# Two graph layers on one core: score chunks moved behind aggregations, masks behind residuals, and a new preparation of the first graph

## The chip, the core and the metric

The kernel runs on one core of a Trainium2 chip. Its engines work side by side and wait for one another by semaphores: TensorE (PE in the profile, its weight loads PEld), VectorE (DVE), ScalarE (ACT), GpSimd (POOL) and SyncE (SP), which issues most of the DMAs. The metric is the time of one execution on the device in microseconds.

## What is computed

Sixteen graphs of 1024 nodes with 256 features go through two layers. The reference, cut to what matters (the adjacency here holds 0 and 1 alone, so that layer 0 uses only `a0`):

```python
# layer 0
e0 = leaky(einsum('bid,bjd->bij', h * a0[:, 0], h))        # leaky: x if x >= 0 else 0.2 x
alpha = sigmoid(where(adj == 1, e0, -max_float))
x = layernorm(h + einsum('bij,bjd->bid', alpha, h) + bias)
# layer 1
Hh = einsum('bni,io->bno', x, W)
logits = (Hh @ a_src)[:, :, None] + (Hh @ a_dst)[:, None, :]
e = where(adj != 0, exp(-leaky(logits)), 0)
x = layernorm(x + elu(einsum('bnm,bmo->bno', e, Hh) / sum(e)))
```

## The kernel before

**Tiles.** A graph's 1024 nodes are 8 tiles t of 128. A product in float32 is made of three products of rounded parts (`split_products`: high x high, low x high, high x low). ScalarE makes the high parts by a rounding copy, GpSimd or VectorE the low parts by a subtraction: `high_x`/`low_x` of x, `high_xT`/`low_xT` of the turned x (its copy scaled by a0 is gT), `high0`/`low0` and `high1`/`low1` of the coefficients of the layers, `keep_H`/`low_H` of the projection.

**Layer 0.** Scores are symmetric, so only the blocks on and above the diagonal are made, in 12 chunks of up to 512 columns (`CHUNKS`): chunks 0 to 2 are rows 7, 6, 5; 3 and 4 row 0; 5 and 6 row 1; 7 and 8 row 2; 9 and 10 row 3; 11 row 4. TensorE makes a chunk in one of two banks (`scores_chunk`), ScalarE writes 0.2 times it (`scale_scores`), VectorE takes the maximum with the bank (`leaky_scores`), ScalarE a tanh over the row (`tanh_row`). The blocks below the diagonal are transposed on TensorE (`mirror`). VectorE forms the coefficients of block t by two kinds of products with the transposed codes: `mask0_below` from the mirrored bank, and `mask0_rest` from `score`. Then high and low part, and `aggregate0`, 24 products of TensorE per tile. The result goes through `residual0`, `stats0`, `moments0` (VectorE), `power0` (GpSimd: variance to 1/sigma) and `norm0` (VectorE), which leaves x1.

**Layer 1.** x1 is turned (`transpose_x1`, `keep_x1T`) and projected (`project`, with two more columns of `W_ext` that hold W a_src and W a_dst). `mask1_tiles` makes the coefficients of several tiles, `aggregate1` sums them, `row_inverse`, `elu_parts` (ScalarE: exponential, then relu), `residual1`, `stats1`, `moments1`, `power1` (GpSimd), `norm1` (ScalarE) and a DMA finish a tile.

**Order.** No scheduler is at work: each engine's instructions stand in the order in which its function `graph(b, prev, nxt)` writes them. Graph 0 and the last one stand by themselves, graphs 1 to 14 run in a loop. Layer 1 of a graph is laced with layer 0's scores of the next, and at the end of graph b ("the border") the masks, high and low parts 0 to 3 of graph b+1 are made between the residuals 4 to 7 of graph b. All semaphores count up; a wait names the count that it needs. Before the first graph there is a preparation: constants, weights, x, the scores of graph 0 and its first four blocks.

The part of the first preparation that makes the two columns of `W_ext` was done on VectorE (`extend_weights`): a product with a row of `a` spread over the partitions (`a_bc`) and a sum, for two columns and two halves.

## Time and profile before

| | us |
|---|---|
| median of 3 runs | 1290.91 |
| lowest, highest | 1290.22, 1291.21 |
| profiled execution, its time | 1292.38 |
| profiled execution, span of its instructions | 1290.6 |
| granted clock of TensorE, mean | 0.992 |

| engine | busy us | share of the span |
|---|---|---|
| PE | 1212.5 | 94% |
| PEld | 1135.5 | 88% |
| POOL | 1045.2 | 81% |
| DVE | 997.1 | 77% |
| ACT | 988.9 | 77% |

The profiled execution's own time is 1.5 us above the median. A row of the timeline gives start, duration, engine, line of the kernel, operation, what it writes and reads with shapes, the number of merged instructions, and in brackets the idle time before it with what ended it. A line is that of a helper, so the tile names tell what it works on: line 1253 is the first of the three products of a step, for scores and aggregations alike.

### The profile page before, as it was taken

How to read it: one execution, taken by the hardware profiler on the slowest of the kernel's cores; microseconds unless marked ns; L12 is line 12 of the kernel's file. 1: busy time of each engine (PE TensorE's matmuls, PEld its weight loads, DVE VectorE, ACT ScalarE, POOL GpSimd, SP SyncE). 2: the span in 40 equal slices, each digit the busy share in tenths (PEclk: the TensorE clock that was granted, in tenths of full speed). 3: DMA queues.
4: the chain of work that ended last, by engine and by line, in shares of the span. 5: the costliest groups of instructions: out<-in, count | busy, mean ns of one | idle time of the engine just before them, and what ended most of it. 6: DMA issues, size and time to landing. Idle time of an engine off the chain costs nothing.

```text
span 1290.6 us, 29789 instructions
## 1 busy us (share of the span) xinstructions
PE 1212.5 (94%) x8898; PEld 1135.5 (88%) x8898; DVE 997.1 (77%) x2499; ACT 988.9 (77%) x2290; POOL 1045.2 (81%) x1052
## 2 busy tenths in 40 slices
PE   5899999999999999999999999999999999999985
PEld 4789899898998989899898988989898898988875
DVE  4678778787877878778787877878778787878855
ACT  4677878778787887878788787887878788787763
POOL 2779797887988889797887988889797887978864
PEclk9999999999999999999999999999999999999988
DMA  9467390854828366381854828366381854818301
GB/s 192 90 118 137 58 178 27 154 106 86 166 40 150 78 131 129 57 164 39 154 106 78 174 37 148 83 129 126 62 162 42 154 106 70 182 34 147 56 9 36
DMA packets 223634, 135.31 MB, mean 105 GB/s; under 512 B 141168, under 2 KB 207088, under 8 KB 223600
## 3 DMA queue, kind: packets, MB, share of 16 engines
q1 hardware_dynamic: 188528, 84.57, 28.0%
q0 software_dynamic: 35072, 50.34, 26.0%
q8 instruction: 15, 0.25, 0.1%
q14 instruction: 19, 0.16, 0.0%
HBM read 101.32 MB, written 16.78 MB: 92 GB/s over the span
## 4 chain that ended last, share of the span: by engine, by line
DVE 34%; POOL 31%; issue 22%; PE 6%; ACT 4%; DVEq 1%; POOLq 1%; DMA 0%; ACTq 0%
POOL coef_lo L394 9%; POOL coef_lo L402 8%; DVE coef L1010 6%; DVE coef L940 5%; POOL rstd L434 3%; DVE stats L1052 3%; DVE reluP L1047 3%; DVE xt_bank L1044 3%; DVE stats L958 2%; DVE coef L931 2%; DVE resid L953 2%; DVE gT_lo L884 2%; POOL var_eps L431 2%; POOL coef_lo L408 2%; POOL h_lo L385 2%
## 5 line engine op out<-in xcount | busy, mean ns | idle before, releaser
L394 POOL TENSOR_TENSOR coef_lo<-coef,coef_hi 128x1024 fp32r<-128x1024 f32 x128 | 307.0, 2405 | 57.4 <-DVE x L970 32.1
L1253 PE MATMUL acc_bank<-h_hi,coef_hi 128*128 128x256 f32 x1024 | 302.5, 295 | 16.6 <-ACT reluP L702 13.9
L402 POOL TENSOR_TENSOR coef_lo<-coef,coef_hi 128x1024 fp32r<-128x1024 f32 (+1 forms) x128 | 294.5, 2308 | 11.5 <-ACT coef_hi L636 11.1
L1253 PE MATMUL acc_bank<-H_hi,coef_hi 128*128 128x258 f32 x1024 | 296.0, 289 | 7.4 <-ACT reluP L702 5.4
L1254 PE MATMUL acc_bank<-H_lo,coef_hi 128*128 128x258 f32 x1024 | 290.6, 284 | 0.0
L1255 PE MATMUL acc_bank<-H_hi,coef_lo 128*128 128x258 f32 x1024 | 290.2, 283 | 0.0
L1255 PE MATMUL acc_bank<-h_hi,coef_lo 128*128 128x256 f32 x1024 | 285.9, 279 | 0.0
L1254 PE MATMUL acc_bank<-h_lo,coef_hi 128*128 128x256 f32 x1024 | 285.8, 279 | 0.0
L1253 PEld LDWEIGHTS acc_bank<-h_hi,coef_hi 128*128 128x128 f32 x1024 | 193.7, 189 | 26.7 <-issue 22.4
L1010 DVE SCALAR_TENSOR_TENSOR coef<-tr_bank,E_col,codeT 128x256 f32<-128x256 f32 (+1 forms) x384 | 193.0, 565 | 24.2 <-POOL coef_lo L402 21.7
L1253 PEld LDWEIGHTS acc_bank<-H_hi,coef_hi 128*128 128x128 f32 x1024 | 194.3, 190 | 11.2 <-issue 8.3
L1254 PEld LDWEIGHTS acc_bank<-H_lo,coef_hi 128*128 128x128 f32 x1024 | 195.1, 191 | 0.6
L1255 PEld LDWEIGHTS acc_bank<-H_hi,coef_lo 128*128 128x128 f32 x1024 | 195.1, 191 | 0.0
L1254 PEld LDWEIGHTS acc_bank<-h_lo,coef_hi 128*128 128x128 f32 x1024 | 193.8, 189 | 1.5
L1255 PEld LDWEIGHTS acc_bank<-h_hi,coef_lo 128*128 128x128 f32 x1024 | 193.2, 189 | 0.0
L626 ACT ACTIVATE coef_hi<-coef 128x1024 fp32r<-128x1024 f32 x128 | 136.2, 1064 | 73.0 <-DVE coef L940 73.0
L588 ACT ACTIVATE score<-lg_bank 128x128 f32<-128x128 f32 (+2 forms) x192 | 94.7, 493 | 86.3 <-PE lg_bank L1255 82.6
L1253 PE MATMUL lg_bank<-hT_hi,gT_hi 128*128 128x384 f32 (+3 forms) x384 | 144.6, 377 | 7.5 <-DVE score L893 4.5
L940 DVE SCALAR_TENSOR_TENSOR coef<-score,codeT 128x512 f32<-128x512 f32 (+1 forms) x192 | 147.9, 797 | 2.0 <-POOL coef_lo L394 0.4
L616 ACT ACTIVATE watch_junk<-codeT,half_cols 128x1024 bf16<-128x1024 bf16 x128 | 147.9, 1155 | 0.6
L1358 PE MATMUL hh_bank<-W_ext,x1T 128*128 128x258 f32 x512 | 139.6, 395 | 7.6 <-ACT x1T L653 4.9
L893 DVE TENSOR_TENSOR score<-lg_bank,score 128x128 f32<-128x128 f32 (+2 forms) x192 | 103.5, 553 | 38.6 <-ACT score L588 38.6
(91 smaller groups left out, 2814.7 us busy)
## 6 DMA issues: line engine op xcount, KB each, us to landing
code_nat<-in_adj POOLq DMA_DIRECT2D x128, 256.0 KB, 4.8
x_raw<-in_x SPq DMA_DIRECT2D x16, 1024.0 KB, 6.5
xb<-bias_bc SPq DMA_DIRECT2D x16, 1024.0 KB, 8.7
xb<-in_x POOLq DMA_DIRECT2D x16, 1024.0 KB, 12.2
out<-x SPq DMA_DIRECT2D x128, 128.0 KB, 2.0
codeT<-code_nat SPq DMA_TRANSPOSE x128, 3.5
W_ext<-in_L_gnn_W SPq DMA_DIRECT2D x1, 256.0 KB, 3.9
x1T<-in_L_gnn_a SPq DMA_DIRECT2D x1, 256.0 KB, 5.1
```

What stands on the lines that cost most here:

```text
L394: nc.gpsimd.tensor_tensor(coef_lo[:, t % 4, :, :], blocks(coef[:, t % 4, :]), f32(coef_hi[:, t % 4, :, :]), ALU.subtract).then_inc(S.lo0, 1)
L402: nc.gpsimd.tensor_tensor(coef_lo[:, t % 4, j0:NT, :], blocks(coef[:, t % 4, j0 * P:N]), f32(coef_hi[:, t % 4, j0:NT, :]), ALU.subtract).t ...
L588: nc.scalar.activation(score_at(J, c0, c1), lg_bank[k % 2][:, 0:(c1 - c0) * P], ACT.Copy, scale=SLOPE).then_inc(F.scaled, 1)
L616: nc.scalar.activation(watch_junk[:, :], codeT[:, t, :], ACT.Square, bias=neg_half[:, :], accum_out=watch_sum[:, t:t + 1]).then_inc(F.code ...
L626: nc.scalar.activation(coef_hi[:, t % 4, :, :], blocks(coef[:, t % 4, :]), ACT.Copy).then_inc(S.hi0, 1)
L893: nc.vector.tensor_tensor(score_at(J, c0, c1), lg_bank[k % 2][:, 0:(c1 - c0) * P], score_at(J, c0, c1), ALU.max).then_inc(F.leaky, 1)
L940: ins = nc.vector.scalar_tensor_tensor(blocks(coef[:, t % 4, j0 * P:j1 * P]), score[:, 0:j1 - j0, at:at + P], 1.0, blocks(codeT[:, t, j0 * ...
L1010: ins = nc.vector.scalar_tensor_tensor(coef[:, at:at + count, J * P:(J + 1) * P], G, E_col[:, J:J + 1], codeT[:, t:t + count, J * P:(J + 1 ...
L1253: nc.tensor.matmul(dst, lhs_hi, rhs_hi, start=first, stop=False)
L1254: nc.tensor.matmul(dst, lhs_hi, rhs_lo, start=False, stop=False)
L1255: return nc.tensor.matmul(dst, lhs_lo, rhs_hi, start=False, stop=last)
L1358: ins = nc.tensor.matmul(hh_bank[:, 0:HC], x1T[:, t % 2, dt, :], W_ext[:, dt, :], start=dt == 0, stop=dt == KD - 1)
```

## The change

It has four parts.

1. **Score chunks.** In layer 1 of graph b, TensorE made chunk 8 behind aggregation 0, chunks 9 and 10 behind aggregation 1 and chunk 11 behind aggregation 2. Now chunks 9, 10 and 11 stand one each behind aggregations 1, 2 and 3. `scale_scores` and `leaky_scores` of them move along.
2. **Masks and high parts at the border.** Row inverse 7 stands behind moments 6, ahead of `mask0_rest` 2; residual 7 ahead of both mask products of block 3. On ScalarE, `high0` 2 and 3 stand behind the relu of tile 7. The high parts of x of the next graph move back by a few places.
3. **Masks 3 and 4 of layer 1's first group** stand behind `norm0` 7 and chunk 2's maximum.
4. **The preparation of the first graph.** x is loaded in three pieces, the last tiles first; the four turned pairs have four banks (`x_bank`) and are not held up by one another; scores start with the first pair. VectorE rounds two of the high parts of x. The columns `a_col` are loaded by ScalarE's queue. W is turned on TensorE and multiplied with both halves of `a` at once (`turn_weights`, `weights_by_a`). The bias is added by GpSimd (`add_bias_pair`) instead of by two DMAs. `mirror` 3 stands behind aggregation 0. The transposing DMAs of codes 4 to 7 stand behind the load of graph 1's x. Two semaphores are merged into others.

The diff, cut to its core (left out: the declarations, waits of the same meaning, `add_bias_pair` and its callers' waits as told above):

```diff
-                    sp.dma_start(a_col[:, k, :], ak.rearrange("(c p) o -> p (c o)", p=P)).then_inc(cols_loaded, 16)
+            for q in range(2):
+                tiles = slice(NT - 2 * q - 2, NT - 2 * q)
+                sp.dma_start(x_raw[:, tiles, :], x_v[0, :, tiles, :]).then_inc(x_part[q], 16)
...
             sp.wait_ge(weights_loaded, 16 * N_WEIGHT_DMAS)
-            sp.sem_inc(past, 1)
-            fill_bias()
+            sp.wait_ge(F.xT, 4)
             sp.wait_ge(F.h_lo, 4)
-            sp.wait_ge(F.xT, 4)
+            sp.wait_ge(F.xb_bias, 4)
             sp.sem_inc(past, 1)
             load_x(F, 1)
+            for t in range(4, NT):
+                turn_codes(0, t, True)
             with sp.Fori(0, LAST - 1) as b:
                 graph(b, True)
...
+            pool.wait_ge(weights_loaded, 16 * N_WEIGHT_DMAS)
+            pool.wait_ge(F.x_loaded, 16)
             for c in range(4):
-                low_x(F, 0, c)
...
-                if nxt:
-                    high_x(F, b + 1, 0)
                 keep_H(F, b, 6, prev, False)
                 keep_x1T(F, b, 7, prev)
-                if nxt:
-                    high_x(F, b + 1, 1)
+                high1_begin(b)
+                if nxt:
                     scale_scores(b + 1, 4)
                 keep_H(F, b, 7, prev, False)
                 ends_H(F, b)
                     scale_scores(b + 1, 6)
...
                         scale_scores(b + 1, 8)
-                        high_x(F, b + 1, 3)
+                        high_x(F, b + 1, 2)
                     if t >= 1:
                         elu_parts(F, b, t - 1)
                     if t == 1:
                         high1(F, b, 4)
                         if nxt:
-                            scale_row(b + 1, 3)
+                            high_x(F, b + 1, 3)
+                            scale_scores(b + 1, 9)
                         high1(F, b, 5)
+                    if nxt and t in (2, 3):
+                        scale_scores(b + 1, 8 + t)
                     if nxt and t == 2:
-                        scale_row(b + 1, 4)
                         tanh_row(b + 1, 0)
                     if t in (3, 4):
                         high1(F, b, t + 3)
-                    if t + 3 >= NT and nxt:
-                        high0(F, b + 1, t + 3 - NT, True)
+                    if nxt and t in (5, 6):
+                        high0(F, b + 1, t - 5, True)
+                    if nxt and t == NT:
+                        high0(F, b + 1, 2, True)
                     if nxt and 3 <= t:
                         tanh_row(b + 1, t - 2)
+                    if nxt and t == NT:
+                        high0(F, b + 1, 3, True)
                     if nxt and t == NT:
                         tanh_row(b + 1, NT - 1)
                     if t in (4, 6, 8):
                         norm1(F, b, t - 4)
                         norm1(F, b, t - 3)
...
             scale_scores(0, 3)
             scale_scores(0, 4)
-            high_x(F, 0, 1)
-            for J in range(4):
-                scale_scores(0, 5 + 2 * J)
-                if J >= 2:
-                    high0(F, 0, J - 2, False)
+            tanh_row(0, 0)
+            scale_scores(0, 5)
+            scale_scores(0, 6)
+            tanh_row(0, 1)
+            for J in range(2, 5):
+                scale_scores(0, 2 * J + 3)
+                high0(F, 0, J - 2, False)
+                if J < 4:
+                    scale_scores(0, 2 * J + 4)
                 tanh_row(0, J)
-                if J < 3:
-                    scale_scores(0, 6 + 2 * J)
-                if J < 2:
-                    high_x(F, 0, J + 2)
-            high0(F, 0, 2, False)
-            tanh_row(0, 4)
...
-                        ins.then_inc(setup_step, 1)
+            def high_x_first(q):
+                dve.wait_ge(x_part[q], 16)
+                tiles = x_pair(F, 0, q)
+                nc.vector.tensor_copy(h_hi[:, tiles, :], x_raw[:, tiles, :]).then_inc(F.h_hi, 1)
+            def keep_W_turned():
+                dve.wait_ge(setup_step, 6)
+                nc.vector.tensor_copy(W_turned, xt_bank[:, :].rearrange("p (c k) -> p c k", c=KD)).then_inc(setup_step, 1)
+            def extend_weights():
+                dve.wait_ge(setup_step, 8)
+                nc.vector.tensor_copy(W_ext[:, :, D:HC],
+                                      hh_bank[:, 0:2 * KD].rearrange("p (c k) -> p c k", c=KD)).then_inc(weights_ready, 1)
             def low_xT(S, b, c, general):
...
                         mask1_tiles(b, 0, 4, 0, 3)
                     if t == 8:
                         low_H(F, b, 5)
-                        mask1_tiles(b, 0, 4, 3, EDGE)
                         keep_watch(b, prev)
                         if prev:
                             keep_range(b - 1)
                     if nxt and 6 <= t:
                         leaky_scores(b + 1, t - 6)
+                mask1_tiles(b, 0, 4, 3, EDGE)
                 if nxt:
                     leaky_scores(b + 1, 3)
                 low_H(F, b, 6)
...
-                    if t >= 3:
+                    if 3 <= t < 7:
                         row_inverse(F, b, t, prev)
-                    if t >= 4 and nxt:
+                    if 4 <= t < 7 and nxt:
                         mask0_below(b + 1, t - 4, True)
+                    if 4 <= t < 6 and nxt:
                         mask0_rest(b + 1, t - 4)
                     residual1(F, b, t, prev)
                     stats1(F, b, t)
                     moments1(F, b, t)
+                    if t == 6:
+                        row_inverse(F, b, 7, prev)
+                        if nxt:
+                            mask0_rest(b + 1, 2)
+                    if t == 7 and nxt:
+                        mask0_below(b + 1, 3, True)
+                        mask0_rest(b + 1, 3)
                     if t < 2:
                         row_inverse(F, b, t + 1, prev)
                     if t == 0:
                         if nxt:
-                            leaky_row(b + 1, 3)
+                            leaky_scores(b + 1, 9)
                         mask1_tiles(b, 6, 2)
-                    if nxt and t == 1:
-                        leaky_row(b + 1, 4)
+                    if nxt and t in (1, 2):
+                        leaky_scores(b + 1, 9 + t)
...
+            high_x_first(1)
             dve.wait_ge(cols_loaded, 16 * KINDS)
-            for c in range(4):
-                low_xT(F, 0, c, False)
-            for J in (7, 6, 5, 0):
-                leaky_row(0, J)
-            dve.wait_ge(weights_loaded, 16 * N_WEIGHT_DMAS)
-            extend_weights(1, D)
+            low_xT(F, 0, 0, False)
+            low_xT(F, 0, 1, False)
+            leaky_row(0, 7)
+            low_xT(F, 0, 2, False)
+            leaky_row(0, 6)
+            low_xT(F, 0, 3, False)
+            leaky_row(0, 5)
+            leaky_row(0, 0)
             leaky_row(0, 1)
-            extend_weights(0, D + 1)
-            for t in range(4):
+            keep_W_turned()
+            mask0_below(0, 0, False)
+            mask0_rest(0, 0)
+            leaky_row(0, 2)
+            extend_weights()
+            for t in range(1, 4):
                 mask0_below(0, t, False)
                 mask0_rest(0, t)
...
+                    if t == 0 and not prev:
+                        mirror(b, 3)
+                        pe.wait_ge(weights_ready, 1)
                     if t >= 2:
                         if t >= 3 or prev:
...
-                    if nxt and 1 <= t < 3:
-                        scores(b + 1, 2 + t)
+                    if nxt and 1 <= t < 4:
+                        scores_chunk(b + 1, 8 + t)
                 if nxt:
                     mirror(b + 1, 3)
...
-                if c >= 2:
-                    pe.wait_ge(F.xT_lo, c - 1)
-                transpose_x(F, 0, c)
+            def turn_weights():
+                pe.wait_ge(weights_loaded, 16 * N_WEIGHT_DMAS)
+                pe.wait_ge(setup_step, 5)
+                for jc in range(KD):
+                    for dt in range(KD):
+                        at = jc * D + dt * P
+                        ins = nc.tensor.transpose(xt_bank[:, at:at + P], W_ext[:, dt, jc * P:(jc + 1) * P], ident[:, :])
+                ins.then_inc(setup_step, 1)
+            def weights_by_a():
+                pe.wait_ge(setup_step, 7)
+                for dt in range(KD):
+                    for jc in range(KD):
+                        ins = nc.tensor.matmul(hh_bank[:, 2 * dt:2 * dt + 2], W_turned[:, jc, dt * P:(dt + 1) * P],
+                                               a_pair[:, jc, :], start=jc == 0, stop=jc == KD - 1)
+                ins.then_inc(setup_step, 1)
+            pe.wait_ge(consts_made, 8)
...
+            scores(0, 5)
             pe.wait_ge(F.xT_lo, 4)
-            for J in (7, 6, 5, 0, 1):
-                scores(0, J)
-            for t in range(4):
-                mirror(0, t)
-                if t < 3:
-                    scores(0, t + 2)
-            pe.wait_ge(weights_ready, 1)
+            scores(0, 0)
+            scores(0, 1)
+            turn_weights()
+            mirror(0, 0)
+            scores(0, 2)
+            weights_by_a()
+            mirror(0, 1)
+            scores(0, 3)
+            mirror(0, 2)
+            scores(0, 4)
             graph(0, False, True)
             with pe.Fori(1, LAST) as b:
```

VectorE in the loop's graph, layer 1 before the change: from row inverse 2 to row inverse 3 (`score` of 128x512 is chunk 11's maximum):

```order
L1036 RECIPROCAL rinv<-rowsum 128x1
L892 REGISTER_ALU
L893 TENSOR_TENSOR score<-lg_bank1,score 128x512
L1044 SCALAR_TENSOR_TENSOR xt_bank<-xt_bank,reluP 128x256
L1047 SCALAR_TENSOR_TENSOR reluP<-xt_bank,x1 128x256
L1052 BN_STATS stats<-reluP 128x6
L1057 BN_AGGR moments<-stats 128x2
L1026 TENSOR_SCALAR rowsum<-acc_bank1 128x1
L1036 RECIPROCAL rinv<-rowsum 128x1
```

The same place in the change:

```order
L1077 RECIPROCAL rinv<-rowsum 128x1
L930 REGISTER_ALU
L931 TENSOR_TENSOR score<-lg_bank0,score 128x256
L1085 SCALAR_TENSOR_TENSOR xt_bank<-xt_bank,reluP 128x256
L1088 SCALAR_TENSOR_TENSOR reluP<-xt_bank,x1 128x256
L1093 BN_STATS stats<-reluP 128x6
L1098 BN_AGGR moments<-stats 128x2
L930 REGISTER_ALU
L931 TENSOR_TENSOR score<-lg_bank1,score 128x512
L1067 TENSOR_SCALAR rowsum<-acc_bank1 128x1
L1077 RECIPROCAL rinv<-rowsum 128x1
```

The maximum of 512 columns moved from before residual 2 to between moments 2 and row sum 3; chunk 10's 256 columns took its place.

VectorE at the end of the loop's graph, before: from the rest of block 2 (`score`, 128x384) over residual 6, row inverse 7 and block 3's two products to residual 7:

```order
L940 SCALAR_TENSOR_TENSOR coef<-score,codeT 128x384
L1044 SCALAR_TENSOR_TENSOR xt_bank<-xt_bank,reluP 128x256
L1047 SCALAR_TENSOR_TENSOR reluP<-xt_bank,x1 128x256
L1052 BN_STATS stats<-reluP 128x6
L1057 BN_AGGR moments<-stats 128x2
L1026 TENSOR_SCALAR rowsum<-acc_bank1 128x1
L1036 RECIPROCAL rinv<-rowsum 128x1
L921 REGISTER_ALU
L930 REGISTER_ALU
L931 SCALAR_TENSOR_TENSOR coef<-tr_bank0,codeT 128x512
L940 SCALAR_TENSOR_TENSOR coef<-score,codeT 128x512
L1044 SCALAR_TENSOR_TENSOR xt_bank<-xt_bank,reluP 128x256
```

The same in the change, from residual 6's moments on:

```order
L1098 BN_AGGR moments<-stats 128x2
L1067 TENSOR_SCALAR rowsum<-acc_bank1 128x1
L1077 RECIPROCAL rinv<-rowsum 128x1
L978 SCALAR_TENSOR_TENSOR coef<-score,codeT 128x384
L1085 SCALAR_TENSOR_TENSOR xt_bank<-xt_bank,reluP 128x256
L1088 SCALAR_TENSOR_TENSOR reluP<-xt_bank,x1 128x256
L1093 BN_STATS stats<-reluP 128x6
L1098 BN_AGGR moments<-stats 128x2
L959 REGISTER_ALU
L968 REGISTER_ALU
L969 SCALAR_TENSOR_TENSOR coef<-tr_bank0,codeT 128x512
L978 SCALAR_TENSOR_TENSOR coef<-score,codeT 128x512
```

The rest of block 2 moved behind row inverse 7, and residual 7 ahead of block 3's two products, after which the loop turns.

## Rows read from the trace of the kernel before

**Rows 1.** The page's part 1: busy us, share, instructions.

```profile
PE 1212.5 (94%) x8898; PEld 1135.5 (88%) x8898; DVE 997.1 (77%) x2499; ACT 988.9 (77%) x2290; POOL 1045.2 (81%) x1052
```

**Rows 2.** Windows: one graph of the loop (7); each engine's busy us (instructions).

```profile
584.10:661.69 77.59, 75.00 (x559) 70.47 (x558) 61.90 (x156) 61.66 (x143) 65.19 (x66) 1.00 0.55 108
```

**Rows 3.** Waits, whole span: us in total, times, longest.

```profile
PE acc_bank L1253 <- ACT reluP L702: 19.4, 30, 1.2
```

**Rows 4.** Timeline of TensorE: transposes of x1 7; A4, A7; N0, N1, N2.

```profile
624.53 0.41 PE L1326 MATMUL xt_bank<-ident,x 128*128 128x128 f32 x2 [0.66 <-DVE x L970]
...
647.73 0.36 PE L1253 MATMUL acc_bank<-H_hi,coef_hi 128*128 128x258 f32 x1 [0.29 <-ACT reluP L702]
...
658.38 0.37 PE L1253 MATMUL acc_bank<-H_hi,coef_hi 128*128 128x258 f32 x1
...
661.69 0.37 PE L1253 MATMUL acc_bank<-h_hi,coef_hi 128*128 128x256 f32 x1
...
666.00 0.36 PE L1253 MATMUL acc_bank<-h_hi,coef_hi 128*128 128x256 f32 x1 [1.00 <-ACT reluP L702]
...
669.87 0.36 PE L1253 MATMUL acc_bank<-h_hi,coef_hi 128*128 128x256 f32 x1 [0.23 <-DVE resid L953]
```

**Rows 5.** Timeline of VectorE: first border's rest of block 0, then graph 7.

```profile
111.51 0.71 DVE L940 SCALAR_TENSOR_TENSOR coef<-score,codeT 128x128 f32<-128x128 f32 x1
...
625.83 0.48 DVE L989 SCALAR_TENSOR_TENSOR H_lo<-hh_bank,scale_col,H_hi 128x256 fp32r<-128x256 f32 x1 [0.38 <-ACT H_hi L677]
...
646.65 0.69 DVE L893 TENSOR_TENSOR score<-lg_bank,score 128x512 f32<-128x512 f32 x1
...
647.69 0.43 DVE L1044 SCALAR_TENSOR_TENSOR xt_bank<-xt_bank,reluP 128x256 f32<-128x256 f32 x1 [0.35 <-ACT reluP L702]
...
649.31 0.16 DVE L1026 TENSOR_SCALAR rowsum<-acc_bank 128x1 f32<-128x1 f32 x1
...
650.64 0.43 DVE L1044 SCALAR_TENSOR_TENSOR xt_bank<-xt_bank,reluP 128x256 f32<-128x256 f32 x1 [0.97 <-ACT reluP L702]
...
653.90 0.35 DVE L940 SCALAR_TENSOR_TENSOR coef<-score,codeT 128x128 f32<-128x128 f32 x1
...
660.54 2.57 DVE L940 SCALAR_TENSOR_TENSOR coef<-score,codeT 128x384 f32<-128x384 f32 x1
...
665.72 1.55 DVE L940 SCALAR_TENSOR_TENSOR coef<-score,codeT 128x512 f32<-128x512 f32 x1
...
669.30 0.42 DVE L953 SCALAR_TENSOR_TENSOR resid<-acc_bank,xb 128x256 f32<-128x256 f32 x1 [0.44 <-PE acc_bank L1255]
```

**Rows 6.** Timeline of GpSimd in the same graph and the next one's begin.

```profile
622.57 0.57 POOL L434 TENSOR_TENSOR rstd<-var_eps,half_cols 128x1 f32<-128x1 f32 x1
...
654.04 2.47 POOL L402 TENSOR_TENSOR coef_lo<-coef,coef_hi 128x1024 fp32r<-128x1024 f32 x1
...
657.95 4.75 POOL L394 TENSOR_TENSOR coef_lo<-coef,coef_hi 128x1024 fp32r<-128x1024 f32 x2
...
668.59 2.38 POOL L394 TENSOR_TENSOR coef_lo<-coef,coef_hi 128x1024 fp32r<-128x1024 f32 x1
...
670.94 0.63 POOL L431 TENSOR_TENSOR var_eps<-moments,eps_cols 128x1 f32<-128x1 f32 x1
```

**Rows 7.** Timeline of ScalarE: exponential of tile 3, two normalisations.

```profile
649.70 0.45 ACT L698 ACTIVATE xt_bank<-acc_bank,rinv 128x256 f32<-128x256 f32 x1 [0.32 <-DVE rinv L1036]
...
659.27 1.08 ACT L708 ACTIVATE x<-reluP,shift,rstd 128x256 f32<-128x256 f32 x2
```

**Rows 8.** Timeline of the preparation, TensorE and VectorE.

```profile
16.55 0.47 PE L1253 MATMUL lg_bank<-hT_hi,gT_hi 128*128 128x128 f32 x1 [2.93 <-DVE gT_lo L884]
...
41.99 0.63 PE L1304 MATMUL tr_bank<-ident,score 128*128 128x128 f32 x4 [2.35 <-ACT score L599]
...
42.37 0.37 PE L1253 MATMUL acc_bank<-h_hi,coef_hi 128*128 128x256 f32 x1
...
26.19 1.53 DVE L867 TENSOR_TENSOR reluP<-W_ext,x1T 128x256 f32<-128x256 f32 x1
```

143 lines of the change are left out of this document (83 added, 60 removed).

## The prediction, made before the changed kernel ran

> **What bounds the kernel now.** I read the engine totals first, then one steady graph in windows, then the waits and the timelines of one border between two graphs. TensorE is busy 1212.5 of 1290.6 us [rows 1], and in one steady graph of 77.59 us it is busy 75.00 [rows 2]. So hardly 2.6 us a graph can be won by removing TensorE's waits, and 14 to 15 graphs share them. The table of waits has one group that matters at the border: aggregations waiting for ScalarE's reluP, 19.4 us in 30 waits [rows 3]. In the timeline the border costs 1.00 us before layer 0's aggregation 1 (I call it N1; layer 1's are A0 to A7, the next graph's layer 0 N0 to N7) and 0.23 before N2, which waits for VectorE's resid; further in, 0.66 before the transposes of x1 tile 7 and 0.29 before A4 [rows 4]. TensorE sets the pace, but VectorE is close behind it there: from A3's row sum to the next graph's first residual it has almost no idle time except where it waits for a relu [rows 5].
>
> The setup is the other piece: the first aggregation starts at 42.37 us, while the first score product starts only at 16.55 [rows 8]. There TensorE is not the bound; a chain over three engines is.
>
> **The setup.** Before, TensorE's first score product waited 2.93 us for the last low part of the turned x [rows 8], since it asked for all four pairs. Now x comes in three pieces, the last tiles first, the four turned pairs have four banks, and row 7's scores need only the first pair. ScalarE's four turns take about 1.4 us each, so do VectorE's. I put the first turn at 6.5 us instead of 8.16 (its columns must still land by the small transfers, now issued by ScalarE), the first score near 9.5, and row 0's first chunk near 14 instead of 21.2: 7 us earlier. VectorE loses the four multiply-reduce pairs that begin with the 1.53 us row [rows 8]; the seven that follow are shorter, and I put the eight at 4.5 us together, in line before the masks of row blocks 0 and 1. The new turn and the two-column product of W cost a 0.7 us copy and a 0.2 us copy there. The last mirror (2.35 us of waiting for tanh [rows 8]) now stands behind the first aggregation: about 1 us more, net of what then becomes late. Sum: 7 + 4.5 - 0.9 + 0.9 = **11.5 us won**. Lower bound 8.5 (the first turn no earlier than 7.5 us, and half of the removed VectorE work in the shadow of other waits); upper 14 (first turn at 5, all removed waits real). The bias is now added by GpSimd in four operations of about 1.3 us (as its low parts of x, of the same size) after those parts; they end near 22 us, before the first coefficient needs it, and the first residual's wait for the DMA goes, behind the aggregations.
>
> **Scores one chunk behind each aggregation.** TensorE does the same products; A3 only starts 1.4 us earlier. A4 waits for relu 2, which hangs on GpSimd's low part 3, then VectorE's eight mask products, residual 1 and row sum 2. None of these moves, so A4 starts at 647.73 again and its 0.29 stays [rows 4]. Nothing is won. But the last leaky maximum, row 4's (0.69 us at 646.65), ran before in the gap in which VectorE waited for relu 2; the next operation began at 647.69 [rows 5]. Now chunk 10's is in that gap, and row 4's stands after moments 2, ahead of row sum 3 (the first order excerpt). Starts of neighbours overlap by 0.09, so row sum 3 moves from 649.31 to 649.91. ScalarE had been idle 0.32 us for that very inverse [rows 7], and VectorE then 0.97 for relu 3 [rows 5]; there is no slack on either. Everything on VectorE down to mask product "rest" of block 0 comes **0.6 us later**: 654.50 instead of 653.90.
>
> **The price of 0.6 us.** Of VectorE's mask products, only the "rest" ones (line 940, score and codeT, both in SBUF) stretch. The one at 660.54 takes 2.57 us and ends 0.41 after the GpSimd pair at 657.95 (4.75 us for two) ends; the one at 665.72 takes 1.55 [rows 5, 6]. Block 0's started at 653.90, 0.14 before GpSimd's last low part of layer 1 (654.04, 2.47 us), took the place between two such operations and was done in 0.35 [rows 5, 6]. GpSimd's times there do not move: its work from low part 1 on is back to back. At 654.50 block 0's rest falls 0.46 into that operation, waits for its end at 656.51 and is done at 656.66: VectorE is 2.4 us late. On from there, all with durations of these rows:
> - residual 4, row inverse 5 and relu 5 end at 659.4; A7 can start at 659.5, not 658.38 [rows 4].
> - block 1's rest meets low part 0 of the next graph and ends at 660.6; ScalarE's high part 1 waits for it and stands with tanh and two normalisations (1.08 us [rows 7]) ahead of relu 6, now 664.0. N0 waits for relu 6: 664.15, not 661.69: +2.5.
> - relu 7 ends at 667.0 and N1 starts at 667.3: here the moved masks do their work, the 1.00 us wait is gone, and the delay falls to 1.3.
> - block 3's rest, behind residual 7, meets low part 2 and ends at 670.9. Residual 0 of the next graph starts at 671.3, not 669.30 [rows 5]; N2 is **2.0 us** late.
> - low part 3 starts at 672.2, not 668.59, and takes 2.4 us again, and the variance step that makes x1 tile 0 stands behind it on GpSimd: 674.6, not 670.94 [rows 6]. So the transposes of x1 tile 0 behind N2 come 3.5 to 3.7 us late, and in the following N3 to N7 TensorE has too little slack to make it good.
>
> I take **3.5 us a border**, with 2.0 (the last step hidden) and 3.7 as bounds. It applies to the 14 borders inside or out of the loop's graphs. At the first one the rest of block 0 began earlier, at 111.51, and took 0.71 instead of 0.28 to 0.35, so it stood some 0.4 to 0.6 us before the gap [rows 5]: 0.6 later it may still come just in time. There I take the intended gain, 0.9 us.
>
> The Trainium skill, page "SBUF — State Buffer", section on the two separate sides, says that GpSimd and VectorE share a port pair as an exclusive lock held for a whole instruction, and that a VectorE operation with two SBUF inputs needs it against a GpSimd operation that reads SBUF. The trace agrees, by the 2.57 us row. If instead both merely slowed each other, the 0.6 us would stay 0.6, and the forecast would be that of rival A.
>
> **Masks 3 and 4 of tile group 0 behind the last norm.** They (1.40 us together, as the next two behind the row of 625.83) leave VectorE's way to x1 tile 7, whose 1/sigma is ready at 623.14 [rows 6]. The transposes at 624.53 start some 0.75 earlier. But low_H 6 then stands behind two masks and the next leaky maximum and ends at 626.35, as before (626.31 [rows 5]), and projection 7 waits for it. Won: 0 to 0.1 us a graph; in the last graph perhaps 0.4. I count 0. The moved high parts of x (0.62 us each on ScalarE) land where it idled 1.0 us or where GpSimd asks for them 2 us or more later: 0.
>
> **Sum** against the profiled execution, 1292.38 us: - 11.5 - 0.9 + 14 x 3.5 = 1329.0; the median of the runs lies 1.5 below the profiled one: **1327 us**.
>
> **Rivals.**
> A. *As meant: the rest of block 0 still slips in.* For it: it needs only 0.4 us less delay than I work out, and the gap is 0.14 wide; an idle microsecond on ScalarE or a shift on GpSimd would do. Against: both sides of the race hang on the same GpSimd chain, whose times repeat in all graphs. Then N1's 1.00 goes, N2 gains less because residual 0 follows block 3's rest: 0.9 a border. 1292.4 - 11.5 - 15 x 0.9 - 1.5 = 1266 (1260 to 1273). This is the faster side; the slow one decides as soon as the rest of block 0 starts after 654.04 in this frame.
> B. *The borders come out even:* the race is lost, but the cascade is short (A7 1.1 late, N0 made good by the 1.00 and 0.23 that go), or won while block 1's rest loses its own race with low part 0 at 657.95 [rows 6]. -0.5 to +1.4 a border: about 1279, 1272 to 1300.
> C. *The setup doesn't shrink:* the transposing DMAs of the codes end too late, since loads of codes and x share the queues. Before, every transpose of codes landed well ahead of its mask; it would have to lose some 8 us against the scores. Price up to 5 us on top of any of the others; inside the range.
>
> **Chances.** Slower as worked out (1303 to 1338): 0.68. A: 0.20. B: 0.12. Likeliest time 1327; its own range 1303 to 1338. The range that holds 8 in 10 leaves out most of A and the top of the first: 1268 to 1336. A difference of 0.2% (2.6 us) is about what a measurement of this kernel can tell. Faster: A and most of B, 0.27; same 0.03; slower 0.70.
>
> **What would show it.** In the profile after: first aggregation near 31 us; a far longer row of block 0's rest (2.0 to 2.5 us instead of 0.35) at the end of graphs 1 to 14; row sum 3 about 0.6 later behind A0; A7 and N0 waiting for reluP; N1 not; the variance step of tile 0 behind a low part; period near 81.1 us. I'm wrong if the period is below 77.6, if that row stays at 0.35, or if the first aggregation starts after 34.

## The result: 4.3% slower, and the profile after

| | before | after |
|---|---|---|
| median of 4 runs each, us | 1291.06 | 1346.41 |
| lowest, highest | 1290.22, 1291.93 | 1343.44, 1347.90 |
| ratio, 95% interval | | 1.0426, 1.0405 to 1.0446 |
| profiled execution, its time | 1292.38 | 1347.90 |
| its span | 1290.6 | 1346.1 |
| first aggregation starts | 42.37 | 31.98 |
| graph 0 (start of its N0 to the next N0) | 77.21 | 80.00 |
| graphs 1 to 14 together | 1085.21 | 1146.32 |
| of these, one graph most often | 77.57 | 81.67 |
| graph 15 to the end of the span | 85.80 | 87.81 |

The direction and the mechanism of the forecast (1327 us) held; its size did not, and the time lies above the range (1268 to 1336). In the profiled execution the change costs 55.5 us: - 10.4 in the preparation, + 2.8 in graph 0, + 61.1 in graphs 1 to 14, + 2.0 behind. A cut at N0 goes through the middle of a border's delay, which is complete only at N3. Cut at N3, it is - 10.4, + 5.3 in graph 0 with the first border (89.12 to 94.45), + 61.0 over the 14 other borders (1086.31 to 1147.28) and - 0.4 behind.

The page's part 1 of the changed kernel (busy us, share, instructions), to be read beside [rows 1]. TensorE has 20.9 us more busy time with nearly the same work, though its share fell. Only a small part of it is the clock (below): graph 7, at full clock in both, has 76.10 us busy for 75.00. What the rest is, no run tells; the ends of products are modelled in these profiles.

```profile
PE 1233.4 (92%) x8910; PEld 1140.4 (85%) x8910; DVE 1034.4 (77%) x2495; ACT 985.6 (73%) x2288; POOL 1056.9 (79%) x1055
```

Its waits of TensorE (us in total, times, longest). The 19.4 us for reluP [rows 3] have become 6.0; the norm of x1 and the mask products "below" have taken their place.

```profile
PE xt_bank L1382 <- DVE x L1011: 30.7, 16, 2.1
PE tr_bank L1360 <- DVE coef L969: 25.7, 30, 1.4
...
PE acc_bank L1309 <- ACT reluP L730: 6.0, 16, 1.6
```

VectorE at the border from graph 7 to 8 of the changed kernel (start, duration, engine, line, operation). A0 starts at 652.12 here and at 631.52 before, so that 20.60 taken off gives the times of [rows 5].

```profile
670.04 0.69 DVE L931 TENSOR_TENSOR score<-lg_bank,score 128x512 f32<-128x512 f32 x1
670.65 0.15 DVE L1067 TENSOR_SCALAR rowsum<-acc_bank 128x1 f32<-128x1 f32 x1
...
675.24 2.04 DVE L978 SCALAR_TENSOR_TENSOR coef<-score,codeT 128x128 f32<-128x128 f32 x1
...
680.27 0.98 DVE L978 SCALAR_TENSOR_TENSOR coef<-score,codeT 128x256 f32<-128x256 f32 x1
...
686.63 0.54 DVE L978 SCALAR_TENSOR_TENSOR coef<-score,codeT 128x384 f32<-128x384 f32 x1
...
690.11 1.46 DVE L978 SCALAR_TENSOR_TENSOR coef<-score,codeT 128x512 f32<-128x512 f32 x1
...
691.49 0.41 DVE L994 SCALAR_TENSOR_TENSOR resid<-acc_bank,xb 128x256 f32<-128x256 f32 x1
...
696.56 0.41 DVE L1011 TENSOR_SCALAR x<-resid,moments,rstd 128x256 f32<-128x256 f32 x1 [0.52 <-POOL rstd L457]
```

GpSimd there, to be read beside [rows 6]: low parts 6 and 7; the next graph's low part 3; the variance step of its tile 0.

```profile
672.37 4.75 POOL L425 TENSOR_TENSOR coef_lo<-coef,coef_hi 128x1024 fp32r<-128x1024 f32 x2
...
692.89 2.40 POOL L417 TENSOR_TENSOR coef_lo<-coef,coef_hi 128x1024 fp32r<-128x1024 f32 x1
695.25 0.64 POOL L454 TENSOR_TENSOR var_eps<-moments,eps_cols 128x1 f32<-128x1 f32 x1
```

Row sum 3 is 0.74 late (650.05 in the old frame for 649.31). The rest of block 0 starts at 675.24, 0.50 behind the start of low part 7 (674.74, half-way in the row of two), and takes 2.04 us instead of 0.35. The variance step of tile 0 ends the row: 3.7 us late against 670.94.

TensorE at the same border: the mirrors before A7 and N0, and the turned x1 tile 0.

```profile
680.15 0.76 PE L1360 MATMUL tr_bank<-ident,score 128*128 128x128 f32 x5 [1.43 <-DVE coef L969]
684.13 0.65 PE L1360 MATMUL tr_bank<-ident,score 128*128 128x128 f32 x4 [0.34 <-DVE coef L969]
...
697.12 0.62 PE L1382 MATMUL xt_bank<-ident,x 128*128 128x128 f32 x2 [2.01 <-DVE x L1011]
```

In graphs 4, 8 and 12 a period is 82.6 instead of 81.7. The windows of graph 8 show why (columns: length, busy us and instructions of PE, PEld, DVE, ACT and POOL, granted clock, DMA share and GB/s): behind the 2.01 us of waiting TensorE is granted 0.57 of its speed on average for 4 us, that is mostly its lower level of 1.2 GHz, and the same products take 0.95 us longer. The same wait in graph 7 had no such fall. In graph 15 the clock falls too, behind a wait of 2.09 us: 0.50 for 4 us, then 0.69 for 4 us (windows 1271 to 1275 and 1275 to 1279).

```profile
694.00:697.00 3.00, 1.10 (x10) 0.90 (x8) 2.48 (x4) 2.97 (x6) 2.44 (x3) 1.00 0.25 87
697.00:701.00 4.00, 3.88 (x16) 3.26 (x17) 3.39 (x10) 3.58 (x8) 1.93 (x3) 0.57 0.00 0
701.00:704.00 3.00, 3.00 (x28) 2.84 (x26) 2.70 (x8) 1.46 (x8) 2.90 (x3) 1.00 0.00 0
```

### The profile page after: what moved, and what is told of

Same layout as the page of the kernel before. It is cut to its first block, busy times and chain, and to the rows that moved or that the text cites. A ratio compares the mean times of both kernels' runs of the same rounds, so it can differ in the third digit from the quotient of the medians.

```text
span 1346.1 us, 29829 instructions
## 1 busy us (share of the span) xinstructions
PE 1233.4 (92%) x8910; PEld 1140.4 (85%) x8910; DVE 1034.4 (77%) x2495; ACT 985.6 (73%) x2288; POOL 1056.9 (79%) x1055
## 4 chain that ended last, share of the span: by engine, by line
POOL 29%; DVE 24%; PE 20%; issue 16%; ACT 8%; DVEq 1%; POOLq 1%; DMA 0%; ACTq 0%
POOL coef_lo L417 9%; POOL coef_lo L425 9%; DVE coef L1051 5%; PE acc_bank L1309 4%; PE hh_bank L1414 4%; PE acc_bank L1311 4%; PE acc_bank L1310 4%; POOL rstd L457 3%; POOL h_lo L402 2%; DVE score L931 2%; ACT coef_hi L654 2%; POOL var_eps L454 2%; DVE coef L978 2%; DVE stats L1093 2%; DVE reluP L1088 2%
## 5 line engine op out<-in xcount | busy, mean ns | idle before, releaser
L978 DVE SCALAR_TENSOR_TENSOR coef<-score,codeT 128x512 f32<-128x512 f32 (+1 forms) x192 | 185.3, 992 | 0.4
L1414 PE MATMUL hh_bank<-W_ext,x1T 128*128 128x258 f32 x512 | 143.9, 404 | 15.2 <-DVE H_lo L1030 9.6
L931 DVE TENSOR_TENSOR score<-lg_bank,score 128x128 f32<-128x128 f32 (+2 forms) x192 | 106.2, 553 | 37.3 <-ACT score L616 36.6
L1311 PE MATMUL lg_bank<-hT_hi,gT_lo 128*128 128x384 f32 (+3 forms) x384 | 132.7, 346 | 0.0
```

The source lines that it names most:

```text
L931: nc.vector.tensor_tensor(score_at(J, c0, c1), lg_bank[k % 2][:, 0:(c1 - c0) * P], score_at(J, c0, c1), ALU.max).then_inc(F.leaky, 1)
L978: ins = nc.vector.scalar_tensor_tensor(blocks(coef[:, t % 4, j0 * P:j1 * P]), score[:, 0:j1 - j0, at:at + P], 1.0, blocks(codeT[:, t, j0 * ...
L1311: return nc.tensor.matmul(dst, lhs_lo, rhs_hi, start=False, stop=last)
L1414: ins = nc.tensor.matmul(hh_bank[:, 0:HC], x1T[:, t % 2, dt, :], W_ext[:, dt, :], start=dt == 0, stop=dt == KD - 1)
```

## The experiments

Fifteen kernels. "Period" is the length of graph 7 of the profiled run; "x1" the start of the norm of the next graph's tile 0 behind A0, at the border before it. Each ratio is against runs of the kernel before made beside it, whose median was 1290.4 to 1291.2.

| kernel | median us | ratio to before, 95% | period | x1 |
|---|---|---|---|---|
| before | 1291 | | 77.59 | 40.71 |
| changed | 1346.41 | 1.0405 to 1.0446 | 81.71 | 44.36 |
| e1 changed, part 1 undone | 1304.06 | 1.0085 to 1.0118 | 78.73 | 41.45 |
| e2 before + part 1 | 1314.56 | 1.0165 to 1.0198 | 79.18 | 42.36 |
| e3 changed, maximum 11 moved | 1308.81 | 1.0117 to 1.0151 | 78.79 | 41.48 |
| e4 before + part 4 | 1285.84 | 0.9948 to 0.9976 | 77.99 | 40.74 |
| e5 changed, variance step ahead | 1343.32 | 1.0392 to 1.0426 | 81.53 | 42.17 |
| e6 e3 + e5 + wait at tile 3 | 1294.84 | 1.0025 to 1.0048 | 78.57 | 39.25 |
| e7 before + border of part 2 | 1306.73 | 1.0104 to 1.0138 | 78.35 | 41.47 |
| e8 e4 + wait at tile 3 | 1285.68 | 0.9948 to 0.9976 | 77.96 | 40.71 |
| e9 e3 + e5 + norm ahead | 1297.17 | 1.0034 to 1.0062 | 78.13 | 39.26 |
| e10 e2, low part 7 waits | 1299.37 | 1.0042 to 1.0077 | 78.36 | 41.48 |
| e11 before + one small operation | 1297.36 | 1.0035 to 1.0063 | 78.17 | 40.77 |
| e12 before + three small ones | 1316.51 | 1.0181 to 1.0210 | 79.53 | 42.25 |
| e13 e9 + turned copy sooner | 1288.30 | 0.9972 to 0.9991 | 77.90 | 39.28 |
| e14 e13 + small pause at tile 3 | 1283.09 | 0.9929 to 0.9962 | 77.78 | 39.29 |
| e15 e4 + small pause at tile 3 | 1284.58 | 0.9934 to 0.9967 | 77.72 | 40.74 |

### Which part costs what (e4, e7, e2, e1)

**e4**, part 4 alone: parts 1 to 3 written back as they were before, on all engines.

> The kernel before with part 4 alone (the new preparation of the first graph; the order in all graphs is that of before). Measures the setup's share: the first aggregation at 32.0 us instead of 42.37, so 10.4 us less: 1280.6 (1279 to 1282). If a part of it were given back in graph 0 (the mirror behind aggregation 0, the transposes of codes 4 to 7 behind the load of x), 1282 to 1286.

The first aggregation starts at 31.37, 11.0 us sooner, but only 5.4 us are left at the end: the loop's graphs take 78.0 instead of 77.6. The prediction had no term for that; it is taken up below.

**e7**, the border of part 2 alone, on the kernel before (VectorE; on ScalarE `high0` 2 and 3 behind relu 7):

```diff
+                    if t == 6:
+                        row_inverse(F, b, 7, prev)
+                        if nxt:
+                            mask0_rest(b + 1, 2)
+                    if t == 7 and nxt:
+                        mask0_below(b + 1, 3, True)
+                        mask0_rest(b + 1, 3)
```

> The kernel before with part 2's order of masks and high parts 0 to 3 at the border alone (row inverse 7 ahead of rest 2, residual 7 ahead of block 3's products, high parts 2 and 3 behind relu 7). Theory 3: the rest of block 0 is in its gap (0.3 us), the 1.00 us before N1 goes and N1, N2 come 1.3 sooner, but block 2's coefficients come 0.5 later, so low parts 2 and 3 on GpSimd 0.75 later and x1 tile 0 with them: period 77.6 + 0.8 = 78.4, in some graphs about 1 more where TensorE's clock falls behind its 2 us wait; 1300 to 1312 us. Intended effect (the wait before N1 is TensorE's only one there): period 76.6, 1276 to 1280.

Part 2 costs 16 us by itself (1290.38 to 1306.73), as theory 3 said and against what the change is for. The 1.00 us before N1 does go (N1 starts 33.23 behind A0 instead of 34.46, N2 36.95 instead of 38.34), but the rest of block 2, now behind row inverse 7, ends 0.5 later, low parts 2 and 3 start at 33.52 and 37.80 instead of 32.82 and 37.06, and the variance step stands behind them.

**e2**, part 1 alone, on the kernel before (TensorE's lines; ScalarE's and VectorE's move along):

```diff
-                    if nxt and 1 <= t < 3:
-                        scores(b + 1, 2 + t)
+                    if nxt and 1 <= t < 4:
+                        scores_chunk(b + 1, 8 + t)
```

> The kernel before with part 1 alone: chunks 9, 10 and 11 one each behind aggregations 1, 2 and 3, nothing else. Theory 1: the period rises by about as much as in the changed kernel (4.1 us) or a little more, since part 2's mask order is not there to take back the 1.00 us before N1: 81.0 to 83; 15 borders x 4.1 = 61 on 1291: 1335 to 1370 us, likeliest 1352. Theory 2 (part 2 is the cause): within 5 us of 1291.

The rest of block 0 loses its place in every graph, but the cost is 23.3 us and not 61: I had put all of the 4.1 us down to part 1.

**e1**, the changed kernel with the same piece turned back:

> The changed kernel with part 1 undone: chunks 9 and 10 behind layer 1's aggregation 1 and chunk 11 behind aggregation 2 on TensorE, their scaled copies and maxima back where they were; parts 2 to 4 stay. Theory 1 (the last leaky maximum, 0.6 to 0.7 us on VectorE ahead of row sum 3, makes the rest of block 0 miss the gap between GpSimd's low parts 6 and 7, and all of the border's loss follows from it): the rest of block 0 takes 0.28 to 0.35 us again in all graphs, the period falls from 81.7 to 77.6 or a little below (76.6 if part 2's gain, the 1.00 us before N1, comes in full), first aggregation still at 32.0; time 1266 to 1282 us, likeliest 1275. Theory 2 (part 2, the moved masks and high parts, costs the border its time, and the longer row of block 0's rest is only a witness): period stays above 80.5, time above 1325.

42 us come back, yet 13 are left, outside both expectations' ranges. The first row is VectorE's rest of block 0, at home again; the second, from TensorE, shows that the 2 us of waiting for x1 tile 0 are there without part 1 too.

```profile
655.73 0.38 DVE L978 SCALAR_TENSOR_TENSOR coef<-score,codeT 128x128 f32<-128x128 f32 x1
```

```profile
596.63 0.41 PE L1382 MATMUL xt_bank<-ident,x 128*128 128x128 f32 x2 [2.01 <-DVE x L1011]
```

The four give a simple account. The period is 77.6, plus the lateness of x1 tile 0 (last column of the table, less 40.71), plus 0.4 in the kernels with part 4: for e1 77.6 + 0.7 + 0.4 = 78.7 (measured 78.7), e2 77.6 + 1.6 = 79.2 (79.2), e7 77.6 + 0.8 = 78.4 (78.4), changed 77.6 + 3.6 + 0.4 = 81.6 (81.7). Where a graph is still longer (e1: 80.1 in three graphs, 79.7 in three), it is the clock behind the 2 us wait: those six graphs have a mean granted clock of 0.98, the others 1.00. The account holds for a late x1; what an early one is worth is another matter (e9).

### The race at the rest of block 0 (e3, e10, e11, e12)

A race here: of a VectorE and a GpSimd operation that get in each other's way, the one that starts a little later waits until the other has ended.

**e3**: the changed kernel, VectorE's maximum of chunk 11 behind row inverse 3; TensorE and ScalarE untouched.

```diff
                     if 3 <= t < 7:
                         row_inverse(F, b, t, prev)
+                    if nxt and t == 3:
+                        leaky_scores(b + 1, 11)
...
-                    if nxt and t in (1, 2):
-                        leaky_scores(b + 1, 9 + t)
+                    if nxt and t == 1:
+                        leaky_scores(b + 1, 10)
```

> The changed kernel with one instruction moved: VectorE's leaky maximum of chunk 11 stands behind row inverse 3, ahead of residual 3, instead of ahead of row sum 3. There VectorE waited 0.97 us for relu 3 before the change. TensorE and ScalarE keep the changed order, so that this tells the place of the maximum from the place of the chunk. Theory 1: row sum 3 and the rest of block 0 are back at their times of before, the rest takes 0.28 to 0.35 us, period 76.6 to 77.7, time 1264 to 1282 us, likeliest 1272. Rival (it is TensorE's chunk behind A3, or ScalarE's copy of it ahead of exponential 3, that delays the border): period above 79.5, time above 1310.

One instruction moved by two places, behind row sum 3 and its inverse, gives 37.6 us back of the 42.4 that undoing part 1 gave: it is the place of the maximum, not TensorE's chunk. Even here one race is lost, at the border behind graph 1 (start 22.75 behind A0, 2.38 us long; at the next 13 borders 22.46 to 22.53 and 0.28 to 0.32). The sum missed for the same reason as e1's.

**e12** and **e11** put no part of the change in, only small operations (a maximum over one column, 0.16 us) ahead of row sum 3 of the kernel before:

```diff
+                if S is F and t == 3:
+                    for k in range(3):
+                        nc.vector.tensor_scalar(pad[:, k:k + 1], acc_bank[1][:, D:D + 1], LEAST_ROWSUM, None, ALU.max)
```

> The kernel before with three such small operations ahead of row sum 3, about 0.3 us in all. Theory 1: the rest of block 0 starts at 22.7, 0.15 behind low part 7's start, and takes 2.3 to 2.5 us; x1 tile 0 comes 1.6 late, period 79.2, time 1311 to 1318 us: 0.3 us of work cost 23 us in the whole. Rival (the lateness grows with the work added, as it would without a lock): 15 x 0.3 = 4.5 us, 1293 to 1297.

> The kernel before with one small VectorE operation more (a maximum over one column, 0.16 us long, but 0.10 from start to start) ahead of row sum 3. The rest of block 0 then starts about 22.48 behind A0, still ahead of low part 7's 22.52. If the gap's edge is where theory 1 puts it (about 0.14 us behind the start of before), this is just in time: rest of block 0 0.3 to 0.4 us, period 77.5 to 77.8, time 1289 to 1294 us. If it is already too late: as the next run, 1313.

The rest of block 0 with three (VectorE, then GpSimd's low parts 6 and 7, which end at 666.52):

```profile
664.18 2.49 DVE L941 SCALAR_TENSOR_TENSOR coef<-score,codeT 128x128 f32<-128x128 f32 x1
```

```profile
661.77 4.75 POOL L403 TENSOR_TENSOR coef_lo<-coef,coef_hi 128x1024 fp32r<-128x1024 f32 x2
```

and with one:

```profile
656.16 0.29 DVE L941 SCALAR_TENSOR_TENSOR coef<-score,codeT 128x128 f32<-128x128 f32 x1
```

With one it starts 22.44 to 22.47 behind A0 and takes 0.28 to 0.35 in every graph of the loop; with three it starts 22.57 to 22.61 and takes 2.5 (22.77 and 2.3 in graph 1). Low part 7 starts at 22.51 to 22.62 in the two. So 0.12 us between the two kernels decide 19 us, and three operations that compute nothing of use cost as much as part 1 (25.6 us for 23.3, of which 5 are the second race, below). The rival, a cost that grows with the work, is out. e11 was not free, though (6.5 us above before); see below.

**e10**: e2, and GpSimd gives way instead of VectorE.

```diff
+                if nxt:
+                    pool.wait_ge(F.mask0, NT * b + NT + 1)
                 low1(F, b, 7)
```

> The second run's kernel (the kernel before with part 1 alone, 1314.56 us, period 79.20) with GpSimd's low part 7 waiting for VectorE's rest of block 0 of the next graph. GpSimd then comes 0.8 us later instead of VectorE 2.1. Theory 1 (the collision costs, not the 0.6 us): the rest of block 0 takes 0.3 to 0.4 us at 23.0 behind A0, low part 7 starts at 23.4, and A7, N0 are not late by more than 0.6: period 77.6 to 78.4, time 1291 to 1304 us. Rival (the 0.6 us and the chunk behind A3 cost the time by themselves, or GpSimd's wait costs as much as VectorE's): period 79 or more, time above 1310.

```profile
656.14 0.28 DVE L943 SCALAR_TENSOR_TENSOR coef<-score,codeT 128x128 f32<-128x128 f32 x1
```

```profile
656.50 2.40 POOL L402 TENSOR_TENSOR coef_lo<-coef,coef_hi 128x1024 fp32r<-128x1024 f32 x1 [0.71 <-DVE coef L943]
```

15 of the 23 us come back (its runs spread from 1295.4 to 1301.4). The delay of 0.6 us is still in this kernel; what is gone is the collision. What is left of the cost comes in the profiled run from another race: the rest of block 2 and GpSimd's low part 1 of the next graph start within 0.02 us of each other. At the border from graph 6 to 7 VectorE loses, from 7 to 8 it wins:

```profile
584.34 2.80 DVE L943 SCALAR_TENSOR_TENSOR coef<-score,codeT 128x384 f32<-128x384 f32 x1
```

```profile
662.70 0.55 DVE L943 SCALAR_TENSOR_TENSOR coef<-score,codeT 128x384 f32<-128x384 f32 x1
```

```profile
584.33 2.39 POOL L394 TENSOR_TENSOR coef_lo<-coef,coef_hi 128x1024 fp32r<-128x1024 f32 x1
```

```profile
662.71 2.80 POOL L394 TENSOR_TENSOR coef_lo<-coef,coef_hi 128x1024 fp32r<-128x1024 f32 x1
```

VectorE loses at 7 of the 15 borders. Each time x1 tile 0 comes 1.3 late (41.5 for 40.2), and the loop's graph behind it takes 78.4 us; behind the 8 borders where it wins a graph takes 77.1 to 77.3, for 77.6 before (graph 1 apart, which had 76.6). So part 1's delay by itself costs a graph of the loop nothing. The spread of the runs would follow if this race fell out differently from run to run; with one trace that is not shown.

### What comes next at the border (e5, e6, e9, e13)

**e5**: the changed kernel with the variance step of tile 0 ahead of low part 3 on GpSimd.

```diff
                 if nxt:
+                    power0(F, b + 1, 0)
                     low0(F, b + 1, 3)
```

> The changed kernel with GpSimd's variance step of the next graph's tile 0 (two operations, 0.63 and 0.88 us) ahead of low part 3 instead of behind it. Nothing else. Theory 3 (from the four kernels so far: the period is that of before plus the lateness of x1 tile 0, whose variance step stands behind low part 3 on GpSimd; plus 0.4 us where the variance step of tile 3 loses to a mask): residual 0 ends at 39.8 behind layer 1's aggregation 0 and its moments at 40.5, so x1 tile 0 can be written near 42.2 instead of 44.4, TensorE's wait of 2.0 us before the transposes goes, low part 3 comes 0.9 later, which N3 can bear: period 79.2 to 80.0 instead of 81.65, and no fall of the clock behind that wait; 1310 to 1322 us, likeliest 1315. Rival (the mirrors' and relu waits before A7 and N0, 1.4 and 0.3 us, set the period alone and x1 tile 0 only follows): period within 0.3 of 81.65 in the undisturbed graphs, time above 1338.

A miss: 3 us instead of 31. **e6** had the same and two more moves (e3's, and the wait of e8):

> The changed kernel with three moves: the leaky maximum of chunk 11 behind row inverse 3 (the third run had it alone, 1308.81), the variance step of tile 0 ahead of low part 3, and VectorE's rest of block 7 waiting for the variance operation of tile 3, so that GpSimd's comes first. Theory 3: N0 at 30.1, N1 at 33.2 and N2 at 37.0 behind A0 as in the third run, x1 tile 0 near 39.2 instead of 41.5, N3 about 2 us sooner, the 0.42 at tile 3 gone: period 76.0 to 76.8, time 1250 to 1266 us, likeliest 1258. Rival (another chain, the coefficients of blocks 3 and 4, is right behind x1 tile 0): period 77.3 to 78.4, 1275 to 1295.

14 us from e3, where I wanted 51. In both, the variance step is in time, and the norm is not; VectorE's row and GpSimd's of e6:

```profile
590.81 2.44 DVE L1012 TENSOR_SCALAR x<-resid,moments,rstd 128x256 f32<-128x256 f32 x1 [0.52 <-POOL rstd L457]
```

```profile
590.74 2.37 POOL L417 TENSOR_TENSOR coef_lo<-coef,coef_hi 128x1024 fp32r<-128x1024 f32 x1
```

Low part 3 has nothing to wait for once 1/sigma is written, and starts 0.07 us ahead of the norm that needs the same value. **e9** makes it wait (it also has e3's move, but not e6's wait):

```diff
                     power0(F, b + 1, 0)
+                    pool.wait_ge(F.x1, NT * b + NT + 1)
                     low0(F, b + 1, 3)
```

> The changed kernel with the leaky maximum of chunk 11 behind row inverse 3, the variance step of tile 0 ahead of low part 3, and low part 3 waiting for x1 tile 0. In the two runs before, the norm of tile 0 stood ready in time but took 2.44 us instead of 0.41: GpSimd's low part 3 had started 0.07 us ahead of it. Theory 4 (any VectorE operation with a float32 tensor of SBUF in and out, this norm too, loses to a GpSimd operation that runs): the norm takes 0.41 at 39.25 behind A0, x1 tile 0 is there at 39.7 instead of 41.7, low part 3 starts at 39.7 (0.6 later), N3 comes near 42.2 instead of 43.9: period 76.8 to 77.3 and time 1262 to 1275 us, likeliest 1268. Rival (block 3's low part is then as late as x1 tile 0 was): period above 78, time above 1285.

The norm takes 0.41, as theory 4 says, and TensorE turns x1 tile 0 2 us sooner. The time did not follow; the rival came out, by another road than it named. TensorE, then ScalarE in e9:

```profile
595.31 0.92 PE L1418 MATMUL hh_bank<-W_ext,x1T 128*128 128x258 f32 x3 [2.05 <-ACT x1T L683]
```

```profile
592.72 1.15 ACT L646 ACTIVATE watch_junk<-codeT,half_cols 128x1024 bf16<-128x1024 bf16 x1
593.77 0.19 ACT L646 ACTIVATION_READ_ACCUMULATOR watch_junk<-codeT,half_cols 128x1 f32 x1
593.87 1.04 ACT L656 ACTIVATE coef_hi<-coef 128x1024 fp32r<-128x1024 f32 x1
594.81 0.36 ACT L683 ACTIVATE x1T<-xt_bank 128x256 f32<-128x256 f32 x1
```

The copy of the turned tile stood behind a watch of codes and high part 4: ScalarE's order was written for a tile 0 that comes late. **e13** puts it ahead:

```diff
+                    if t == 1:
+                        keep_x1T(F, b, 0, prev)
                     if t < 6:
                         watch_codes(b, t)
```

> The kernel of the ninth run (1297.17 us, period 78.1) with ScalarE's copy of the turned x1 tile 0 ahead of the watch of codes 1 and of high part 4, behind both of which it stood (it waited from 10.2 to 12.2 behind aggregation N0, and TensorE's projection 2.05 us for it). Theory 5 (the period hangs on the chain x1 tile 0, turned copy, projection, N3): N3 comes 1.2 to 1.6 sooner, then bounded by low part 3 (42.2 behind A0); period 76.5 to 76.9 in all graphs, with no fall of the clock, 1263 to 1274 us. Rival (aggregations 4 to 7 wait for their coefficients and eat it up): period 77.5 or more, 1285 or more.

9 us, and the first kernel with all the parts that is not slower than before. N3 starts 42.27 behind A0 (43.75 in e9), the promised 1.5; but N4 gains 0.4 of it, N7 0.2 and the next A0 0.2: the rival, too. The projection of tile 1 waits 0.79 us for ScalarE's next copy in turn.

### The second race (e8, e15, e14)

e4, e8, e11 and e12 take 0.36 to 0.45 us longer from N4 to N7 (e4 14.57 us, before 14.20). In the kernel before, GpSimd's variance operation of tile 3 started 0.04 us ahead of VectorE's rest of block 7; graph 7, GpSimd and VectorE:

```profile
605.14 0.19 POOL L431 TENSOR_TENSOR var_eps<-moments,eps_cols 128x1 f32<-128x1 f32 x1
```

```profile
605.18 1.29 DVE L940 SCALAR_TENSOR_TENSOR coef<-score,codeT 128x512 f32<-128x512 f32 x2
```

In e4 it is the other way round, and an operation on one column takes as long as the product over 512. Why the two starts change places is not shown: none of part 4, e11's or e12's edits stands near them, and they differ by less than 0.1 us. The rows of e4:

```profile
596.72 0.69 POOL L454 TENSOR_TENSOR var_eps<-moments,eps_cols 128x1 f32<-128x1 f32 x1
```

```profile
596.66 0.69 DVE L974 SCALAR_TENSOR_TENSOR coef<-score,codeT 128x512 f32<-128x512 f32 x1
```

**e8** tried a wait:

```diff
+                    if t == 4:
+                        dve.wait_ge(F.var0, NT * b + 4)
                     if 1 <= t and t + 3 < NT:
                         mask0_rest(b, t + 3)
```

> The kernel before with part 4 alone (1285.84) and one wait more: VectorE's rest of block 7 waits for GpSimd's variance operation of tile 3. With part 4 that operation took 0.69 us instead of 0.19 in the loop's graphs, since VectorE's product started at 21.09 and the variance operation at 21.14; before it was 21.08 against 21.04. Theory 3: it takes 0.19 again, the period falls from 78.0 to 77.6, 14 x 0.42 = 5.9 us less: 1279 to 1282 us. Rival (the period of part 4 is longer for another reason, such as the places of instructions in memory): within 1.5 us of 1285.8.

The variance operation takes 0.19 again and nothing is won. That told nothing against the theory: VectorE's product now starts 0.43 later (21.52 behind N0, for 21.09), and the norm of tile 3 behind it at 22.73, as late as in e4 (22.83; before 22.29). **e15** has in place of the wait two increments of a semaphore that nobody reads.

> The kernel before with part 4 alone (1285.84 us, period 77.97) and the same two increments between moments 3 and the rest of block 7. Theory (the order of the variance operation and the mask decides 0.4 us a graph): the variance operation takes 0.19 us, the mask starts less than 0.1 behind it, the norm of tile 3 starts at 22.3 instead of 22.8 behind N0; period 77.55 to 77.65, time 1279 to 1282 us. Rival (something else of part 4 lengthens the loop): 1285 or more.

GpSimd and VectorE in e15:

```profile
596.76 0.19 POOL L454 TENSOR_TENSOR var_eps<-moments,eps_cols 128x1 f32<-128x1 f32 x1
```

```profile
597.02 0.69 DVE L974 SCALAR_TENSOR_TENSOR coef<-score,codeT 128x512 f32<-128x512 f32 x1 [0.34 <-POOL coef_lo L417]
```

The period falls by 0.27 of the 0.40; the product is 0.26 behind the variance operation, more than wanted, and the norm of tile 3 starts at 22.60. The total gains only 1.3 us on e4, and the two intervals overlap: graphs 0, 1 and 15 gave back 2.8. From N4 to N7, summed over graphs 1 to 14, e15 gives back 3.2 of the 5.0 us that e4 had lost there, and e14 2.5 against e13. That the order of the two decides 0.2 to 0.3 us a graph is shown; the whole of the 0.4 is not. And it costs only where nothing hides it: in e9 the variance operation takes 0.69 too, but N3 and N4 start 0.4 later behind N0 than in e4, and N4 to N7 takes 14.24.

**e14** has the same pause on e13:

> e13 with two semaphore increments (no work) on VectorE between moments 3 and the rest of block 7, so that GpSimd's variance operation of tile 3 starts first and VectorE's mask a little behind it, as in the kernel before. If the order there costs 0.4 us a graph also here: 5 to 6 us less than e13, 1258 to 1268. If N4 to N7 have slack enough now: the same as e13 within 1 us.

It is 5.2 us faster than e13: about 0.25 a graph, and 2.5 in graph 1, where e13's rest of block 0 lost its race at 22.73 and e14's does not. At 1283.09 us e14 beats both kernels, by 0.6% and 4.7%. It can't be told apart from e15 (1284.58, runs from 1282.4 to 1285.2), which has nothing of parts 1 to 3.

## Why the prediction was right and where it was wrong

**The setup: 11.5 forecast, 10.4 measured.** The two terms were wrong in opposite ways. ScalarE's first turn started at 8.07, not 6.5, held up 3.56 us by the transfers of `a_col`, which ScalarE's queue now issues; the first score came at 11.03 (9.5 forecast), row 0's first chunk at 16.37 (14): 4.8 won, not 7. From there to the first aggregation 15.6 us instead of 21.2 [rows 8]: 5.6 won, for 4.5.

```profile
8.07 0.60 ACT L590 ACTIVATE hT_hi<-lg_bank 128x512 fp32r<-128x512 f32 x1 [3.56 <-DMA a_col<-in_L_gnn_a]
```

**The 0.6 us and its price, right.** Row sum 3 came 0.74 late, the rest of block 0 ended 2.4 late as worked out, and e3, e10, e11 and e12 show that it is the collision that costs. The Trainium skill, page "SBUF — State Buffer", section on the two separate sides, says just that: the pair of ports is locked for a whole instruction, and the other engine fully blocks. By that rule the 2.5 us of e12 are expected and the 0.29 of e11 too; the traces agree.

**The cascade, right in its end, wrong on the way.** N0 + 2.5 (forecast 2.5), N1 + 1.4 (1.3), N2 + 1.6 (2.0), variance step of tile 0 + 3.7 (3.66). A7 came 1.7 late, not 1.1: the mirrors of block 2 need a bank that VectorE's product "below" of block 1 must have read, and wait 1.43 us ahead of A7. I had followed reluP alone. It did no harm to the sum, since x1 tile 0 sets the period.

**The size: 19 us too low.** Against the profiled execution I had 1329.0 and it took 1347.9. Four terms were off:

| term | forecast | measured | miss |
|---|---|---|---|
| setup | - 11.5 | - 10.4 | 1.1 |
| first border (start of N0 of graph 0 to N3 of graph 1) | - 0.9 | + 5.3 | 6.2 |
| 14 borders (from there to N3 of graph 15) | + 49.0 | + 61.0 | 12.0 |
| from there to the end | 0 | - 0.4 | - 0.4 |

The step that failed at the 14 borders is "I take 3.5 us a border" as the whole of what a graph loses. N3 came 3.65 late (46.96 behind A0 for 43.31), so that the cascade was worked out well: 14 x 0.15 = 2.1 of the 12.0. But an undisturbed graph, N3 to N3, takes 4.07 us longer: the other 0.42, in all 5.9, had no term. N4 to N7, where the second race stands, make 3.8 of them, and the variance operation of tile 3 takes 0.69 here as well (graph 7; VectorE's product starts at 625.30):

```profile
625.35 0.69 POOL L454 TENSOR_TENSOR var_eps<-moments,eps_cols 128x1 f32<-128x1 f32 x1
```

How much of the 5.9 the order of these two decides was not run on this kernel. The falls of the clock behind the 2 us wait, in graphs 4, 8, 12 and 15, had no term either: 3 x 0.95 + 1.0 = 3.9. The three make 11.9. The second race can be seen in the trace of before, but only to someone who looks for VectorE and GpSimd starting within 0.04 us of each other. In graph 15 N4 to N7 came 4.2 us later behind N0, for x1 tile 0 and the clock; by its A0 2.7 was left.

**The first border: here the step that failed is "0.6 later it may still come just in time".** The rest of block 0 starts there at 22.02 behind A0 and takes 0.71 [rows 5]; I read the length as slack. It was waiting for low part 6 to end at 22.6, so that its slack was a little over 0.5, and 0.60 was taken (row sum 3 at 18.31 behind A0 for 17.71). In the changed kernel it and low part 7 both start at 102.10, and it loses; x1 tile 0 comes 4.9 late there (44.34 behind A0 for 39.40):

```profile
102.10 2.53 DVE L978 SCALAR_TENSOR_TENSOR coef<-score,codeT 128x128 f32<-128x128 f32 x1
```

**Rival A was no rival.** I gave 0.20 to the change working as meant, at 0.9 us a border. e7 has the race won in all graphs and is 16 us slower than before, and e1, the changed kernel with the race won, 13 us: the moved rest of block 2 makes low parts 2 and 3 0.7 late, and the norm of tile 0 behind them. I had seen that chain in the losing case and left it out of the winning one; "N2 gains less" was not the point, since x1 tile 0 and not N2 sets N3. With it, the forecast would have had no faster side worth 0.27. Rival C did not come: the first aggregation starts at 31.98, 1.1 us later than forecast.

**Masks 3 and 4 behind the last norm: counted at 0.** Their gain is not seen: the projection of tile 7 waits 0.54 us for H_lo 6 instead (17 waits for H_lo of 9.6 us in all), as the forecast said of low_H 6. No run had this part alone. **A4** kept its 0.29 (0.31 now), and so did the order of everything up to row inverse 2.

## What to carry to other kernels

Where two engines share a lock, look in the trace not only at the long rows but at pairs of starts within a few tenths of a microsecond, and price the loss of each such race separately: 0.12 us decided 19 us here, and four such places stood in one graph (the rests of blocks 0 and 2, the variance operation of tile 3, the norm of tile 0). A wait that is taken away has a use only if the chain behind it comes sooner too: write down who releases the next three steps of the bounding engine before counting a gain. And a new order that makes one chain earlier leaves the other engines' orders written for the old one; e9 and e13 each found the next instruction in the way.

## What the runs showed of the hardware

- Which of two operations goes first can hang on 0.02 us: in e10 the same two start within it at 14 borders, and VectorE's product takes 0.55 or 2.80 us.
- The collision works both ways: VectorE's product over 512 columns held GpSimd's operation on one column for 0.69 us instead of 0.19.
- The norm, a tensor_scalar with one float32 tensor of 256 columns in SBUF, result in SBUF and two columns as scalars, loses too: 2.44 us behind a low part that started 0.07 ahead, 0.41 without. I had counted only products of two tensors in SBUF. Whether its mode or its scalar columns make it so, no run tells.
- The granted clock fell to the lower level behind a wait of 2.0 us in some graphs and not in others: in 3 of the 14 loop graphs of the changed kernel (and in its last graph), in 6 of e1's. In e13 and e14, where that wait is gone, no graph shows it at that place.
